# Two operand loads a step, one with a repeated source, in place of eight

## The reference

```python
# attention half, of y = layernorm(x)
y_h = y.reshape(b, t, 16, 8).transpose(0, 2, 1, 3)
scores = einsum('bhtk,bhsk->bhts', y_h, y_h) / sqrt(8)
attn = softmax(scores, axis=-1)
o = einsum('bhts,bsc->bhtc', attn, y)          # 16 heads x 128 channels
x = x + layernorm(o.transpose(0, 2, 1, 3).reshape(b, t, 2048) @ weight)
# second half, of z = layernorm(x), z_prev = z shifted by one position
r = sigmoid((mu_r * z + (1 - mu_r) * z_prev) @ W_r.T)
k = relu((mu_k * z + (1 - mu_k) * z_prev) @ W_k.T) ** 2
x = x + layernorm(r * (k @ W_v.T))
```

## Time and profile before

| | |
|---|---|
| median of 3 runs | 1006.61 us (1005.31 to 1006.96) |
| profiled execution | 1009.22 us |
| its span | 1007.4 us |
| mean granted TensorE clock | 0.978 |
| TensorE matmul busy | 913.3 us (91%) |
| VectorE busy | 867.4 us (86%) |
| ScalarE busy | 750.8 us (75%) |
| GpSimd busy | 327.2 us (32%) |
| casts, share of the 16 DMA engines | 69.0% |
| SyncE's queue, share of the 16 DMA engines | 14.0% |

### The profile page before, as it was taken

The page is one execution under the profiler, slowest core; times in us unless marked ns, Lnnn a source line. Parts: engine busy times, 40 slices in busy tenths (PEclk is TensorE's granted clock), DMA queues, the critical chain, the costliest instruction groups (busy, mean ns, idle before and its releaser), DMA issues.

```text
span 1007.4 us, 17595 instructions
## 1 busy us (share of the span) xinstructions
PE 913.3 (91%) x5930; PEld 437.1 (43%) x5930; DVE 867.4 (86%) x1112; ACT 750.8 (75%) x1028; POOL 327.2 (32%) x513
## 2 busy tenths in 40 slices
PE   1699999999999999989999999999999999999932
PEld 1244444444444444444444444444444444444521
DVE  6889998989799998798898899979989988989942
ACT  2577877877877787868878768786887878787731
POOL 1112321451144421633126521345116331255121
PEclk9999999999999999999999999999999999999975
DMA  5699999889898879898888888898988998989700
GB/s 175 148 209 184 205 193 207 194 192 200 175 183 169 177 156 187 190 209 180 171 180 162 177 166 172 176 215 178 189 172 171 198 188 164 181 177 189 142 11 11
DMA packets 100346, 174.42 MB, mean 173 GB/s; under 512 B 21537, under 2 KB 62881, under 8 KB 100257
## 3 DMA queue, kind: packets, MB, share of 16 engines
q0 software_dynamic: 36864, 134.23, 69.0%
q1 hardware_dynamic: 63200, 38.93, 14.0%
q10 hardware_dynamic: 192, 0.13, 0.1%
HBM read 28.51 MB, written 10.49 MB: 39 GB/s over the span
## 4 chain that ended last, share of the span: by engine, by line
PE 54%; POOL 12%; DVE 10%; issue 8%; ACT 8%; DMA 4%; SPq 3%; POOLq 0%; DVEq 0%; ACTq 0%
PE ps_o L443 14%; PE ps_o L445 13%; PE ps_o L444 13%; POOL fnw L291 9%; PE ps_s L426 5%; ACT e_f L537 5%; DVE e_lo L747 4%; DMA e_hi<-e_f 3%; PE ps_r L458 2%; PE ps_r L457 2%; PE ps_r L456 2%; POOL e_hi L326 2%; POOL nw L291 1%; SPq L232 1%; SPq L230 1%
## 5 line engine op out<-in xcount | busy, mean ns | idle before, releaser
L747 DVE TENSOR_TENSOR e_lo<-e_f,e_hi 128x2048 f16<-128x2048 f32 x256 | 584.3, 2282 | 53.3 <-DMA e_hi<-e_f 52.4
L537 ACT ACTIVATE e_f<-ps_s 128x2048 f32<-128x2048 f32 x256 | 481.7, 1881 | 142.2 <-PE ps_s L426 134.7
L443 PE MATMUL ps_o<-e_hi,y_hi 128*128 128x512 f16 x1024 | 391.9, 383 | 11.4 <-DVE o_neg L753 11.2
L445 PE MATMUL ps_o<-e_hi,y_lo 128*128 128x512 f16 x1024 | 389.5, 380 | 0.0
L444 PE MATMUL ps_o<-e_lo,y_hi 128*128 128x512 f16 x1024 | 389.4, 380 | 0.0
L326 POOL DMA_DIRECT2D e_hi<-e_f x256 | 140.5, 549 | 609.2 <-ACT e_f L537 546.6
L549 ACT ACTIVATE part<-ps_r,rden 128x128 f32<-128x128 f32 x512 | 145.4, 372 | 48.3 <-DVE rden L759 48.3
L443 PEld LDWEIGHTS ps_o<-e_hi,y_hi 128*128 128x128 f16 x1024 | 99.9, 98 | 161.2 <-issue 63.4
L445 PEld LDWEIGHTS ps_o<-e_hi,y_lo 128*128 128x128 f16 x1024 | 100.4, 98 | 121.8 <-issue 1.5
L444 PEld LDWEIGHTS ps_o<-e_lo,y_hi 128*128 128x128 f16 x1024 | 100.6, 98 | 92.1 <-issue 2.0
L426 PE MATMUL ps_s<-op_t,op_s 32*128 32x512 f16 x1024 | 102.0, 387 | 25.3 <-ACT e_f L537 16.0
(11 more groups left out here) (133 smaller groups left out, 447.6 us busy)
## 6 DMA issues: line engine op xcount, KB each, us to landing
e_hi<-e_f POOLq DMA_DIRECT2D x256, 512.0 KB, 5.0
op_t<-scr_t SPq DMA_DIRECT2D x508, 32.0 KB, 3.6
op_s<-scr_s SPq DMA_DIRECT2D x512, 16.0 KB, 3.5
scr_s<-yT SPq DMA_DIRECT2D x12, 256.0 KB, 4.9
scr_t<-yT SPq DMA_DIRECT2D x12, 256.0 KB, 4.6
xs<-in_L_attn_x_dram SPq DMA_DIRECT2D x4, 512.0 KB, 7.3
out_dram<-res SPq DMA_DIRECT2D x8, 256.0 KB, 5.3
scr_s<-eighth SPq DMA_DIRECT2D x4, 256.0 KB, 3.2
```

The lines of the kernel that those rows point to most:

```text
L443: nc.tensor.matmul(dst, y_hi[:, b % 2, s, :], e_hi[:, ring, g, :], start=(q == 0 and g == 0), stop=False)
L445: mm = nc.tensor.matmul(dst, y_lo[:, b % 2, s, :], e_hi[:, ring, g, :], start=False, stop=(q == 1 and g == 3))
L537: nc.scalar.activation(e_f[:, k % EF_RING], ps_s[:], ACT.Exp, scale=1.0 / ROOT).then_inc(weighed, 1)
L747: dve.tensor_tensor(flat(e_lo[:, ring]), flat(e_f[:, k % EF_RING]), flat(e_hi[:, ring]), ALU.subtract).then_inc(split, 1)
```

## The change

`op_s_load` and `op_t_load` lose their argument `g`, and each describes the load of all 128 partitions. The destination is `op_s[:, slot, :]` or `op_t[:, slot, :]`. The source of `op_s` is a view with the group outermost: 4 groups, 32 rows, 256 columns. The source of `op_t` is the view of 32 rows and 512 columns, with a dimension of 4 and step zero put ahead of it. So a step issues two DMAs on SyncE's queue, and step 0 has one of them on ScalarE's. `score` waits for 32 a step where it waited for 128. The bytes, the rows, the rings and the places of the loads in the order stay.

```diff
--- before.py
+++ after.py
@@ -179,17 +179,18 @@
         def batch_of(j):
             return j // (2 * H)
 
-        def op_s_load(j, g):
+        def op_s_load(j):
 
             rows = slice(j % H * HS, (j % H + 1) * HS)
-            return (op_s[32 * g:32 * g + 32, j % OP_RING, :],
-                    scr_s[batch_of(j)][rows, :, 2 * g * P:(2 * g + 2) * P].rearrange("k i t -> (k i) t"))
-
-        def op_t_load(j, g):
+            return (op_s[:, j % OP_RING, :],
+                    scr_s[batch_of(j)][rows].rearrange("k i (g t) -> g (k i) t", g=4))
+
+        def op_t_load(j):
 
             th, rows = j // H % 2, slice(j % H * HS, (j % H + 1) * HS)
-            return (op_t[32 * g:32 * g + 32, j % OP_RING, :],
-                    scr_t[batch_of(j)][rows, :, th * BANK:(th + 1) * BANK].rearrange("k i t -> (k i) t"))
+            return (op_t[:, j % OP_RING, :],
+                    scr_t[batch_of(j)][rows, :, th * BANK:(th + 1) * BANK].rearrange("k i t -> (k i) t")
+                    .unsqueeze(0).to_broadcast([4, 4 * HS, BANK]))
 
         LAST = QUADS + LAG + 4 + SPAN
 
@@ -226,10 +227,9 @@
                 ge(sp, scored, 2 * (j - OP_RING + 1))
                 if j % (2 * H) == 0:
                     sp.wait_ge(scr_in[batch_of(j)], 7 * 16)
-                for g in range(4):
-                    sp.dma_start(*op_s_load(j, g)).then_inc(op_in[slot], 16)
-                    if j > 0:
-                        sp.dma_start(*op_t_load(j, g)).then_inc(op_in[slot], 16)
+                sp.dma_start(*op_s_load(j)).then_inc(op_in[slot], 16)
+                if j > 0:
+                    sp.dma_start(*op_t_load(j)).then_inc(op_in[slot], 16)
 
             keep_hi(0)
             keep_lo(0)
@@ -419,7 +419,7 @@
                 j, q = k // 2, k % 2
                 slot = j % OP_RING
                 if q == 0:
-                    pe.wait_ge(op_in[slot], 128 * (j // OP_RING + 1))
+                    pe.wait_ge(op_in[slot], 32 * (j // OP_RING + 1))
                 ge(pe, weighed, k)
                 for g in range(4):
                     here = slice(32 * g, 32 * g + 32)
@@ -598,8 +598,7 @@
             take_y(0, 1)
             take_shift(0)
             act.wait_ge(scr_in[0], 7 * 16)
-            for g in range(4):
-                act.dma_start(*op_t_load(0, g)).then_inc(op_in[0], 16)
+            act.dma_start(*op_t_load(0)).then_inc(op_in[0], 16)
             for k in range(LAST):
                 if k < QUADS:
                     weigh(k)
```

## The result

The changed kernel takes 1053.2 us (median of 4) against 1006.8: a ratio of 1.0449, with a 95% interval of 1.0419 to 1.0479. It is slower by 46 us. The forecast was 1097 us, 91 us slower, in a range of 1015 to 1165. The direction is right, the amount is twice too large.

What follows compares the result with a forecast made beforehand. TensorE bound the kernel at 7.19 us a step; after the change engines 0 to 3 would, at 7.83. That costs 82 us, plus 9 at batch boundaries: 91 us slower, 1097 us, range 1015 to 1165.

Steps and rivals of the forecast that it cites:

- the mean DMA share and TensorE's pace leave little room: Mid-kernel, TensorE sets the pace at 7.19 us a step, with DMA engines 80 to 90% busy and not far behind.
- the loads run on four engines: Each new load, with 4 outermost in its source, uses four DMA engines: 128 + 4 packets on ACT's queue.
- they are the same four for every load: All loads use the lowest-numbered engines, 0 to 3, taken from the Trainium skill; no run had shown it.
- the 10 named: At batch boundaries, the wait at L228 for a batch's writes grows from up to 6.3 us to over 10.
- the saved issuing gives at most 3.6 us: Six fewer issues a step on SyncE give at most 2.6 us early plus 1 at the start; forecast as nothing.
- The sum: Work of one loaded engine a step: casts 5.43, loads 2.60 plus 0.03 completions, rest 0.24, together 8.30 us.
- 1.06: Busy reading of the fullest stretch, 43 to 60 us, used as divisor: 8.30 us becomes 7.83 a step.
- The term of the loads: On each of four engines a step, 64 rows at 40.6 ns are 2.60 us, plus 0.03 for completions.
- The 9 us for batch boundaries: New batches' loads wait for writes queued behind loads on the four engines: 3 us, three times.
- The second rival: Four engines carry the loads but keep up with 7.19 us a step: 1007 to 1022 us, chance 0.10.
- A wait of TensorE's L426: TensorE's wait for loaded operands, 8.9 us before, grows to tens of us, while casts land near 5 to 6.

Runs made afterwards that it cites:

- only_s: Kernel before with only op_s loaded by one DMA (four engines), op_t by four DMAs as before; 1009.6 us, ratio 1.0016.
- only_t: Kernel before with only op_t loaded by one DMA (four engines), op_s by four DMAs as before; 1023.3 us, ratio 1.0137.
- layout_s_const: Kernel before with op_s as one sixteen-engine load from re-laid scratch, op_t still four loads, a batch's constant row written by one DMA; 1003.5 us, ratio 0.9968.
- two_engines: Changed kernel with four loads a step, 2 outermost in the source, so two engines carry all loads; 1314.0 us, ratio 1.3019.
- half_t: Changed kernel without the op_t load of every second step from step 5 on, leaving out half of those loads; 1023.8 us, ratio 1.0170.
- after_lag5: Changed kernel with one quad more between scores and products, rings of e_f and e_hi/e_lo one deeper; 1056.2 us, ratio 1.0468.
- two_dmas_16: Changed kernel with its two loads over sixteen engines, from re-laid scratch needing 28 writes a batch in place of 7; 1060.2 us, ratio 1.0487.

## Why the prediction was right in its sign and twice too large

**Point by point.** That the mean DMA share and TensorE's pace leave little room held: 0.96 us of `op_s` on an engine is hidden (`only_s`), 1.49 us of `op_t` is not (`only_t`). That the loads run on four engines held exactly: 132 packets on q10, and 15,300 fewer on q1 plus 60 on q10 are the 15,360. That they are the same four for every load no view shows by engine; on changing ones an engine's mean work would be 6.4 us a step as before, and the slices above would not stand at four and at two. The DMA share dropped while the time grew, as forecast. The longest wait for a batch's last write is 14.0 us, over the 10 named. How late the loads land can't be said. That the saved issuing gives at most 3.6 us was tested only in part: `layout_s_const` saves three of eight issues and gains 3 us.

**The size.** The sum had 8.30 us of readings a step and divided by 1.06; the rows after have 8.07. The term of the loads was over-sized, 2.63 against 2.44 (41.1 ns a row with its completion against 38.2), the casts by 0.04. And the loaded engines read more than 1.06: 1.07 here, 1.10 in `two_engines`. With 7.54 in place of 7.83 us a step, that is 0.29 x 127.5 = 37 us. The 9 us for batch boundaries don't show: SyncE's wait for the last write of a batch rose by 7 us in all, 19.7 to 26.6, but TensorE has no wait for operands at any boundary. 37 + 9 = 46 covers the 45 that are missing. The factor is read from the result, so this books the error rather than derives it: the prediction took its divisor from one stretch of 17 us in which the loads were a tenth of the reading, and that more loads overlap more with casts is the likely reason, which no run isolates.

Part of it is also that the sum compared means. Work on a loaded engine in a step, estimated by the prices above (for the kernel before by the prediction's), and the pace measured:

| kernel | work, us | pace, us | work / pace | time, us (ratio) |
|---|---|---|---|---|
| before | 6.43 | 7.19 | 0.89 | 1006.8 (1) |
| only_s | 7.02 | 7.17 | 0.98 | 1009.6 (1.0016) |
| half_t | 7.34 | 7.29 | 1.01 | 1023.8 (1.0170) |
| only_t | 7.42 | 7.28 | 1.02 | 1023.3 (1.0137) |
| after | 8.07 | 7.54 | 1.07 | 1053.2 (1.0449) |
| two_engines | 10.49 | 9.53 | 1.10 | 1314.0 (1.3019) |

The threshold is soft. The time rises before the mean says full, and so does the number of slices with four engines' worth of work (65, 67, 140 and 263 for before, only_s, only_t and after). That stretches differ in pace (above, 100 to 400 us against 400 to 700) is the likely reason, and it was only argued. Then the engines fill up further as the work grows. The second rival, four engines that keep up, is nearly right for one load, and wrong for two.

**The step that failed.** "A wait of TensorE's L426 for `op_t` or `op_s` becomes the largest, casts keep a landing near 5 to 6 us, because an engine with both queues waiting serves them in turn", and SyncE's wait for `scored` would vanish or turn into long issues. The reverse happened: the casts land at 7.2 us, there is no wait for operands after the first 40 us and SyncE waits 618.5 us, though some issues are long as well (up to 10.3 us). The likely reason, argued and not tried by a run: the loads go out the moment a slot is free, four steps ahead, while a cast has to be back within some quads and isn't done before its slowest engine is. So the short loop pays for what the long one takes. Only with two engines, where the loads alone are 4.88 us, are both late. That the order in which an engine serves the two queues has a part in this was not tried. The prediction named this outcome as one that would prove it wrong; it was wrong in who waits, and right in which engines are full.

Not settled: how much of the 46 us is the queueing of casts in front of a nearly full engine and how much is the engine's capacity. `after_lag5`, `two_engines` and the slices with hardly any idle time speak for capacity; that `only_t` already costs 14 us at 1.02 speaks against capacity alone.

## What to carry to other kernels

Read a load's packets, not its bytes: rows plus completions tell how many DMA engines it uses, and an outermost dimension of 4 in the source made it four. The Trainium skill, *DMA: Bandwidth & Descriptors*, section "Rules for kernel authors", asks for an outermost dimension that is a multiple of 16, and this case agrees: with the same two loads a step took 7.54 us on four engines and 7.20 on sixteen. When transfers concentrate on a few engines, compute the work of those engines, everything that is spread over all sixteen included, and expect to see the delay at the transfer with the shortest deadline, not at the one that was changed. Fewer DMAs bought 3 us here, and a layout that needs more writes cost 40 in the queue that issues them.

## What the runs showed of the hardware that was not expected

The busy shares of two queues on the same engines add up to more than 100%: 94.3 + 11.4%, and by the estimates above 1.07 to 1.10 on the loaded engines. In a burst of writes of 64 and 256 KB on SyncE's queue an issue takes about 2 us (`two_dmas_16`, 447 to 486 us), where single ones took 0.32 to 0.43 us at 18 to 26 us of the changed kernel, with no casts in flight. In the changed kernel one issue of `op_s` took 10.3 us on SyncE's queue and one of `op_t` 6.1:

```profile
L230 SPq DMA_DIRECT2D op_s<-scr_s x128: 509/510/10262, 27.8 to 964.0; - x128
...
L232 SPq DMA_DIRECT2D op_t<-scr_t x127: 510/767/6088, 29.2 to 964.6; - x127
```

After 6 us without a matmul, in `two_dmas_16`, TensorE ran for 5.5 us at the lower level of its clock (0.50).
